# Two interleaved recurrences: the expert layer on blocks of 8 steps, half the lead, and the next stage's first weights spread earlier

## The reference, cut to what matters

```python
def cell(h, x):                                  # layer 1, 256 steps, 8 batches
    gi = x @ W_ih + b_ih; gh = h @ W_hh + b_hh
    r = sigmoid(i_r + h_r); z = sigmoid(i_z + h_z); n = tanh(i_n + r * h_n)
    return (1 - z) * n + z * h
# layer 1's experts, on every h: 8 experts of rank 16, the best one alone
base = h @ W_base.T + b_base;  e = argmax(h @ router_W.T)
x = x + base + 2.0 * B[e] @ (A[e] @ h)
# layer 2, 256 steps: four evaluations a step (Runge-Kutta)
dq = q - q**3/3 - p + x_t + tanh(q) @ coupling.T + bias
dp = EPSILON * (q + ALPHA - BETA * p)
# layer 2's retrieval: 64 of 4096 experts for each row
z = silu((h . down_embed[idx]) * softmax(score));  x = x + sum_k z_k * up_embed[idx_k]
```

## Time and profile before

| | us |
|---|---|
| median of 3 runs | 5199.05 (5195.85 to 5218.25) |
| the profiled execution, its own time | 5227.58 |
| its span, first to last instruction | 5225.8 |
| PE busy | 4851.0 (93%) |
| DVE busy | 2831.0 (54%) |
| ACT busy | 1520.9 (29%) |

### The profile page before, as it was taken

One profiled execution on the slowest core, in us unless ns is written; L12 is line 12 of the kernel. 1 busy time (PEld: TensorE's weight loads), 2 busy tenths in 40 slices (PEclk: granted clock), 3 DMA queues, 4 the chain that ended last, 5 costly groups with the idle time before them and its releaser, 6 DMA issues. The chain is left out here.

```text
span 5225.8 us, 196853 instructions
## 1 busy us (share of the span) xinstructions
PE 4851.0 (93%) x83712; PEld 3836.6 (73%) x83712; DVE 2831.0 (54%) x16413; ACT 1520.9 (29%) x6006; POOL 280.7 (5%) x859
## 2 busy tenths in 40 slices
PE   7899999799999999999996699999989998999978
PEld 3344654589999999999996588799889997344433
DVE  3211011379999999999997635675544341444411
ACT  1100111234444444444443223233322221333310
POOL 0010010001111111111111000000000000000000
PEclk7699999655555555555555599999989999899989
DMA  2201431000000000000001000033400000000000
GB/s 80 101 34 41 165 140 35 14 4 5 5 5 5 5 5 5 5 5 5 5 5 51 13 9 2 34 87 93 128 14 3 3 3 34 11 16 17 12 21 32
DMA packets 54335, 163.72 MB, mean 31 GB/s; under 512 B 13873, under 2 KB 18097, under 8 KB 48192
## 3 DMA queue, kind: packets, MB, share of 16 engines
q1 hardware_dynamic: 47456, 134.89, 7.7%
q0 software_dynamic: 3712, 12.29, 0.7%
q10 hardware_dynamic: 2304, 4.20, 0.2%
HBM read 129.63 MB, written 17.17 MB: 28 GB/s over the span
## 5 line engine op out<-in xcount | busy, mean ns | idle before, releaser
L616 PE MATMUL k_ps<-k_hl,k_wlo 128*128 128x8 f16 x16384 | 606.6, 169 | 141.0 <-ACT k_hl L692 135.9
L616 PEld LDWEIGHTS k_ps<-k_hl,k_wlo 128*128 128x128 f16 x16384 | 532.9, 105 | 178.2 <-ACT k_hl L692 160.6
L620 PE MATMUL k_ps<-k_hl,k_whi 128*128 128x16 f16 x16384 | 588.6, 174 | 0.0
L620 PEld LDWEIGHTS k_ps<-k_hl,k_whi 128*128 128x128 f16 x16384 | 516.1, 104 | 0.6
L616 PE MATMUL g_ps<-g_hl,g_wlo 128*128 128x8 f16 x12288 | 436.7, 168 | 43.2 <-DVE g_hl L770 38.2
L620 PE MATMUL g_ps<-g_hl,g_whi 128*128 128x16 f16 x12288 | 441.5, 174 | 0.0
L616 PEld LDWEIGHTS g_ps<-g_hl,g_wlo 128*128 128x128 f16 x12288 | 387.1, 104 | 49.4 <-DVE g_hl L770 43.6
L692 ACT ACTIVATE k_hl<-k_q 128x32 f16<-128x32 f32 x768 | 176.2, 229 | 742.9 <-DVE k_q L727 742.9
L620 PEld LDWEIGHTS g_ps<-g_hl,g_whi 128*128 128x128 f16 x12288 | 387.1, 104 | 0.0
L1441 DVE TENSOR_REDUCE t_NM<-t_ps 128x1 f32<-128x512 f32 x256 | 165.1, 686 | 218.2 <-PE t_ps L1310 218.2
L1213 DVE TENSOR_TENSOR HQ<-p_ior,p_pm 128x2048 f32<-128x2048 f32 x64 | 146.3, 2290 | 223.7 <-PE p_sim L1037 223.7
(11 more groups left out here) (326 smaller groups left out, 8960.7 us busy)
## 6 DMA issues: line engine op xcount, KB each, us to landing
GRZ<-expert_places SPq DMA_DIRECT2D x64, 512.0 KB, 4.9
wm<-in_w_dram SPq DMA_DIRECT2D x4, 2816.0 KB, 10.4
GRZ<-in_w_dram SPq DMA_DIRECT2D x4, 2816.0 KB, 9.8
m_w<-in_w2a_dram SPq DMA_DIRECT2D x8, 1280.0 KB, 12.7
GRZ<-in_ue_dram SPq DMA_DIRECT2D x8, 1024.0 KB, 8.4
XT<-in_xT_dram SPq DMA_DIRECT2D x1, 4096.0 KB, 12.5
GRZ<-in_x_nat_dram SPq DMA_DIRECT2D x4, 1024.0 KB, 18.8
expert_rows<-wm SPq DMA_DIRECT2D x1, 4096.0 KB, 23.7
```

The source lines that it names most:

```text
L616: T.matmul(P[:,j,1,:],lo[:,kc,(m0+j)*128:(m0+j+1)*128],x[:,kc,0,:],start=(j==0 and kc==0),stop=False,skip_group_check=True)
L620: i=T.matmul(P[:,j,:,:],hi[:,kc,(m0+j)*128:(m0+j+1)*128],x[:,kc,:,:],start=False,stop=kc==KC-1,skip_group_check=True)
```

## The change

The constants become LEAD = 16 and TL = 8. A block of the experts is then 8 steps, 64 rows; there are 32 blocks in place of 16, and each must be through in 8 steps. PE takes four float32 matmuls (eight instructions) a step at i = 0 to 5, where it took two at i = 0 to 11. The matrices in the weights' place stay 128x128 for the base and B matmuls, which now have 64 moving columns; the rank matmuls have 64 weight columns and 136 moving ones. DVE's expert choice moves to i = 1 and 2, its writes of 128x64 to i = 6 and 7, ACT's scaling to i = 3. Step 8(j+1)-16, the first to need block j, comes one step after i = 7; before, it came three steps after i = 13.

In the retrieval tile 0's four is-equal matrices get places of their own (`B0`, in memory that is free by then), so that `weights_hot(0)` is issued on DVE after tile 12's picks, `pairs_hot(0)` after tile 13's, and `pairs_hot(1)` to `(3)` between the last tile's products; PE issues `scatter(0,q)` behind `pick(15,q)`, and ACT `spread(0,q)` there. In the first tile of the second half PE's order becomes `combine(0,q); scatter(1,q)` in place of `scatter(1,q); combine(0,q)`. DVE builds tile 1's matrices in the order 5, 6, 7, 4, then `weights_hot(1)`.

```diff
-LEAD, TL = 32, 16
+LEAD, TL = 16, 8
...
-                if i<2:
-                    if i==0:
-                        e.wait_ge(g_h,TL*(j+1))
...
-                    for d in (2*i,2*i+1):
-                        x=T.matmul(psh[:,0:136],hs[:,d,:],ar[:,d,:],start=d==0,stop=d==3)
-                    if i==1: x.then_inc(l_h,1)
-                if i==2: e.wait_ge(l_x,4*j)
-                if 2<=i<10:
-                    for u in (2*(i-2),2*(i-2)+1):
-                        dc,d=u//4,u%4
-                        T.matmul(pso[:,dc*128:(dc+1)*128],wb[:,d,dc*128:(dc+1)*128],hs[:,d,:],start=u==0,stop=False,skip_group_check=True)
-                if i==4:
+                if i==0:
+                    e.wait_ge(g_h,TL*(j+1))
...
+                    for d in range(4):
+                        x=T.matmul(psh[0:NE,0:136],hs[:,d,:],ar[:,d,:],start=d==0,stop=d==3)
+                    x.then_inc(l_h,1)
+                if i==1: e.wait_ge(l_x,4*j)
+                if 1<=i<5:
+                    dc=i-1
+                    for d in range(4):
+                        T.matmul(pso[:,dc*NE:(dc+1)*NE],wb[:,d,dc*128:(dc+1)*128],hs[:,d,:],start=dc==0 and d==0,stop=False,skip_group_check=True)
+                if i==2:
                     e.wait_ge(l_ht,j+1)
-                    T.transpose(pst[:,0:128],ht[:],K.ident[:]).then_inc(l_tr,1)
-                if i in (10,11):
+                    T.transpose(pst[:,0:NE],ht[0:NE,:],K.ident[0:NE,0:NE]).then_inc(l_tr,1)
+                if i==5:
                     e.wait_ge(l_hm,j+1)
-                    for dc in (2*(i-10),2*(i-10)+1):
-                        x=T.matmul(pso[:,dc*128:(dc+1)*128],bw[:,dc*128:(dc+1)*128],hm[:],start=False,stop=True,skip_group_check=True)
-                    if i==11: x.then_inc(l_o,1)
+                    for dc in range(4):
+                        x=T.matmul(pso[:,dc*NE:(dc+1)*NE],bw[:,dc*128:(dc+1)*128],hm[:,0:NE],start=False,stop=True,skip_group_check=True)
+                    x.then_inc(l_o,1)
...
-                elif i in (12,13):
-                    dc=2*(i-12)+part
+                elif i in (6,7):
+                    dc=2*(i-6)+part
...
+        B0=[x.rearrange('p (j r) -> p j r',r=128) for x in (wm[:,4096:6144],R[:,0:2048],R[:,2048:4096],HF[:,0:2048])]
...
                     pick(i,q)
                     dense(i+1,2*q+1)
+                    if i==NTL-1: scatter(0,q)
...
-            for q in range(4): scatter(0,q)
             for i in range(NTL):
                 for q in range(4):
-                    scatter(i+1,q)
+                    if i>=1: scatter(i+1,q)
                     combine(i,q)
+                    if i==0: scatter(1,q)
...
+                    if i==NTL-1: spread(0,q)
...
                     product(4*i+q)
                     rows_hot(4*i+4+q)
+                    if i==NTL-1 and q<3: pairs_hot(q+1)
...
+                if i==NTL-4: weights_hot(0)
+                if i==NTL-3: pairs_hot(0)
-            for q in range(4): pairs_hot(q)
-            weights_hot(0)
-            for q in range(3): pairs_hot(4+q)
+            for q in range(1,4): pairs_hot(4+q)
+            pairs_hot(4)
             weights_hot(1)
-            pairs_hot(7)
```

More of the change, by code:

```diff
@@ L591, in scan @@
         view=lambda P: P[:,0:64].rearrange('p (m s b) -> p s m b',m=KC,s=2)
-        R_,Z_,N_=range(3)
+        R_,Z_,N_=range(3); NE=TL*NB
         a,h=DT/2,DT
@@ L632, in experts @@
                 hs=HS[:,j%2].rearrange('p d t b -> p d (t b)')
-                if i<2:
-                    if i==0:
-                        e.wait_ge(g_h,TL*(j+1))
-                        if j==0: e.wait_ge(s_lw,64)
-                    for d in (2*i,2*i+1):
-                        x=T.matmul(psh[:,0:136],hs[:,d,:],ar[:,d,:],start=d==0,stop=d==3)
-                    if i==1: x.then_inc(l_h,1)
-                if i==2: e.wait_ge(l_x,4*j)
-                if 2<=i<10:
-                    for u in (2*(i-2),2*(i-2)+1):
-                        dc,d=u//4,u%4
-                        T.matmul(pso[:,dc*128:(dc+1)*128],wb[:,d,dc*128:(dc+1)*128],hs[:,d,:],start=u==0,stop=False,skip_group_check=True)
-                if i==4:
+                if i==0:
+                    e.wait_ge(g_h,TL*(j+1))
+                    if j==0: e.wait_ge(s_lw,64)
+                    for d in range(4):
[7 more added lines that the diff above has]
+                if i==2:
                     e.wait_ge(l_ht,j+1)
-                    T.transpose(pst[:,0:128],ht[:],K.ident[:]).then_inc(l_tr,1)
-                if i in (10,11):
+                    T.transpose(pst[:,0:NE],ht[0:NE,:],K.ident[0:NE,0:NE]).then_inc(l_tr,1)
+                if i==5:
                     e.wait_ge(l_hm,j+1)
-                    for dc in (2*(i-10),2*(i-10)+1):
-                        x=T.matmul(pso[:,dc*128:(dc+1)*128],bw[:,dc*128:(dc+1)*128],hm[:],start=False,stop=True,skip_group_check=True)
-                    if i==11: x.then_inc(l_o,1)
+                    for dc in range(4):
+                        x=T.matmul(pso[:,dc*NE:(dc+1)*NE],bw[:,dc*128:(dc+1)*128],hm[:,0:NE],start=False,stop=True,skip_group_check=True)
+                    x.then_inc(l_o,1)
             for s in range(LEAD):
@@ L680, in masked @@
                 j,i=s//TL-1,s%TL
-                if i!=5 or j<0 or j>=NT//TL: return
-                e.wait_ge(l_tr,j+1); A.activation(hm[:],pst[:,0:128],ACT.Copy,scale=2.0).then_inc(l_hm,1)
+                if i!=3 or j<0 or j>=NT//TL: return
+                e.wait_ge(l_tr,j+1); A.activation(hm[:,0:NE],pst[:,0:NE],ACT.Copy,scale=2.0).then_inc(l_hm,1)
             scaled(0)
@@ L777, in experts @@
                 if j<0 or j>=NT//TL: return
-                if i==2 and part==0:
+                if i==1 and part==0:
                     e.wait_ge(l_h,j+1)
-                    at['mx']=ch.did(V.tensor_reduce(mx[:],psh[:,128:136],AX.X,ALU.max))
-                elif i==2:
[L782 to L787, removed]
+                    at['mx']=ch.did(V.tensor_reduce(mx[0:NE,:],psh[0:NE,128:136],AX.X,ALU.max))
+                elif i==1:
+                    ch.after(at['mx'])
+                    at['mk']=ch.did(V.scalar_tensor_tensor(mk[0:NE,:],psh[0:NE,128:136],mx[0:NE,0:1],io[0:NE,:],ALU.is_ge,ALU.mult))
+                elif i==2 and part==0:
+                    ch.after(at['mk'])
+                    at['ix']=ch.did(V.tensor_reduce(ix[0:NE,:],mk[0:NE,:],AX.X,ALU.min))
+                elif i==2:
                     ch.after(at['ix'])
-                    V.scalar_tensor_tensor(ht[:],io16[:],ix[:,0:1],psh[:,0:128],ALU.is_equal,ALU.mult).then_inc(l_ht,1)
-                elif i in (12,13):
-                    dc=2*(i-12)+part
+                    V.scalar_tensor_tensor(ht[0:NE,:],io16[0:NE,:],ix[0:NE,0:1],psh[0:NE,0:128],ALU.is_equal,ALU.mult).then_inc(l_ht,1)
+                elif i in (6,7):
+                    dc=2*(i-6)+part
                     e.wait_ge(l_o,j+1)
                     x=XT[:,dc,:,j*TL:(j+1)*TL].rearrange('p b t -> p t b')
-                    V.scalar_tensor_tensor(x,pso[:,dc*128:(dc+1)*128].rearrange('p (t b) -> p t b',b=NB),bb[:,dc:dc+1],x,ALU.add,ALU.add).then_inc(l_x,1)
+                    V.scalar_tensor_tensor(x,pso[:,dc*NE:(dc+1)*NE].rearrange('p (t b) -> p t b',b=NB),bb[:,dc:dc+1],x,ALU.add,ALU.add).then_inc(l_x,1)
             e.wait_ge(s_c,32)
@@ L1036, in scatter @@
                         for h in range(2):
-                            x=T.matmul(psw[b][n%2][h*64:(h+1)*64,j*32:(j+1)*32],Bp[b*64:(b+1)*64,q,j,h*64:(h+1)*64],AW[b*64:(b+1)*64,q*16+j,:],start=True,stop=True)
+                            hot=B0[q] if i==0 else Bp[:,q]
+                            x=T.matmul(psw[b][n%2][h*64:(h+1)*64,j*32:(j+1)*32],hot[b*64:(b+1)*64,j,h*64:(h+1)*64],AW[b*64:(b+1)*64,q*16+j,:],start=True,stop=True)
                 x.then_inc(s_W,1)
@@ L1125, in _ @@
             weight(NTL-1)
-            for i in range(NTL):
+            for i in range(1,NTL):
                 for q in range(4): spread(i,q)
@@ L1210, in pairs_hot @@
                 i,q=n//4,n%4
-                if i>=1: e.wait_ge(s_W,n-3)
-                else: e.wait_ge(s_t,4*NTL-3+q)
-                V.tensor_tensor(Bp[:,q],bc(ior[:].unsqueeze(1),[128,16,128]),bc(PM[:,i,1,q*16:(q+1)*16].unsqueeze(2),[128,16,128]),ALU.is_equal).then_inc(s_bp,1)
+                if i==0 and q>=1: e.wait_ge(s_t,4*NTL-3)
+                if i==1: e.wait_ge(s_t,4*NTL)
+                if i==1 and q==0: e.wait_ge(s_W,4)
+                if i>=2: e.wait_ge(s_W,n-3)
+                V.tensor_tensor(B0[q] if i==0 else Bp[:,q],bc(ior[:].unsqueeze(1),[128,16,128]),bc(PM[:,i,1,q*16:(q+1)*16].unsqueeze(2),[128,16,128]),ALU.is_equal).then_inc(s_bp,1)
             def weights_hot(i):
```

## The result

The changed kernel is slower: 5287.59 us median against 5204.41 for the kernel before, measured beside it, ratio 1.016 (95% interval 1.0134 to 1.0186). The forecast was +67 us, to 5266 (5238 to 5302); the medians differ by 83.2.

A forecast was written before the change was run, and what follows sets the result against it. The oscillator's chain was taken to set the scan step, with PE's slot already full. Lead -66.7, new blocks +169, old blocks -18 and retrieval -17 gave +67 us, to 5266 us (5238 to 5302).

The forecast's parts named there:

- The full slot: PE's gap behind the oscillator's fourth evaluation: 0.92 us of room, filled by four instructions (0.99); any more is paid in full.
- The price of an instruction: Expert float32 matmuls in the scan: weight columns set the cost, so it stays 0.213 us at 64 columns and the number doubles.
- the cheap rival: Expert instructions in the scan cost 0.107 us at 64 columns, as moving columns alone would have it; total 5115; chance 0.07.
- The block's excess: Extra time of each new 8-step expert block over steps free of experts: 5.4 us, from 5.0 to 6.1.
- eight narrow instructions: A scan slot holding eight expert instructions lengthens its step by 0.75 to 0.86 us, taken as 0.80.
- The rank portion: Expert instructions at i = 0 of a block, 136 columns at 0.227 us each: 0.88 to 0.98 us extra.
- the transpose: The one PE transpose in each expert block of the scan: 0.21 us extra, as in step 69 before.
- The lead: Sixteen GRU-alone and sixteen oscillator-alone scan steps become sixteen joint ones: 66.7 us gained.
- Waits of POOL: POOL's drive waits for x only one step ahead in the scan; slack covers it, costing nothing, else up to 1 us a block.
- The retrieval: New order in the retrieval brings scatter(2,0) 17 us nearer to the scan's end, from 14 to 20.
- the two later holes: PE gaps of about 5 us in the retrieval that may drop the clock; first combine 8.65 us against some 7.4.
- The sum: Whole kernel: scan +84 and retrieval -17 give +67 us on the median of 5199.05.

The follow-up runs named there:

- half_count: The changed kernel with half of the base matmuls left out, four instructions a slot at i = 1 to 4: scan 2009.7 us against 2106.7.
- half_columns: The changed kernel with base matmuls moving 32 columns in place of 64, half the product left out: scan 2099.1 us against 2106.7.
- wide_transpose: The changed kernel with the transpose of all 128 rows of ht in place of 64: scan 2100.4 us against 2106.7.
- lead32_tl8: The changed kernel with LEAD = 32 and TL = 8, the lead as before: scan 2162.8 us against 2106.7.
- late_ue: The changed kernel with the first four up-embedding pieces issued after two of the last tile's four picks: retrieval 1413.4 us against 1414.0.
- later_ue: The changed kernel with the first four up-embedding pieces issued only after all the last tile's picks: retrieval 1411.6 us against 1414.0.
- lead30_order: The kernel before with LEAD = 30, the changed retrieval, up-embeddings issued behind all picks, and scatter(1,3) ahead of combine(0,3): 5184.97 us, ratio 0.9944.

## Why the prediction was right

The result lies in the range and on the forecast's side, and the mechanism is the one forecast. That the scan's +84 came so near to +84.9 is in part luck: two errors of almost 6 us cancel, as the third step shows. By its steps:

- **The full slot.** Right. half_count takes four instructions out of four slots a block and gets back 97 us.
- **The price of an instruction, 0.213 us at 64 columns.** Right, read from L396 and L117. This was the step on which the sign hung, and the cheap rival fell to half_columns. Its size is twice 128 columns at 1.2 GHz (0.107 us), not once.
- **The block's excess, 5.4 us.** A touch low: steps one to seven of a block stand at 8.34, 8.07, 8.44, 8.03, 8.03, 8.10 and 7.35 in the median (over 7.26), and with the free step the block's excess is 5.6. The 31 new blocks then cost 174.7 us, where I had 167 and 2 for block 0; but the old ones, taken out, had cost 23.6 and not the 18 I took (nor my bound of 23), and -66.2 + 174.7 - 23.6 is 84.9. Of the terms, eight narrow instructions cost 0.75, the bottom of my bounds and not the 0.80 I took. The rank portion cost 1.08 in place of at most 0.98, and the transpose 0.41 in place of 0.21. Both have 64 rows or columns of weights, and I had priced them as if the array size did not matter; wide_transpose shows this for the transpose, and for the rank portion it is argued.
- **The lead, -66.7.** Right: lead32_tl8 forecast 2164 with it, and measured 2162.8. Without the experts' excess the two profiles give -66.2.
- **Waits of POOL.** Right; 0.73 us of slack or more was left.
- **The retrieval, -17.** Mis-sized; it was -6.3. The chain behind it was right (the bare passes over AW cost 4.7 and the clock 2.7), but the step "2 us each" for the scatters between the last picks was wrong. A pick or a scatter takes 2.1 us at the full clock and took 3.6 at the lower one. Up to the last pick that is 7.6 us more, for half a pick, two picks and two scatters, and the hole took 3.2: together 10.8 for the 10.7 by which scatter(1,0) was late. I had allowed for the lower clock in the two later holes alone, and for no hole of PE's own.
- **The sum.** +67 against +83.2 on the medians and +78.6 in the profiles; what is missing in the profiles is the retrieval's 11 us, and the other 4.6 of the medians are no more than executions scatter.

## What to carry to other kernels

Ask of a matmul what it pays for before you cut it up: a float32 instruction with a full set of weights cost 0.213 us at the lower clock with 128, 64 and 32 moving columns alike, so a block of half the rows costs the same and there are twice as many. A shorter lead-in is gained once, while what it takes to allow it is paid in every block: here 56 us once against 141. And where work is packed in the gaps of a full engine, look at the one slot it lands in, not at the busy share.

## What the runs showed of the hardware

- A float32 transpose with 64 rows of weights among full matmuls costs more than a full one: 0.35 + 0.30 us against 0.21 + 0.21 (wide_transpose).
- A row of eight narrow float32 instructions pays for fewer columns once, at its ends, and not eight times: 0.05 us for 32 columns fewer (half_columns).
- PE stopped for 2.8 to 3.2 us with work in hand while the DMA engines were busy with the up-embeddings (the change, late_ue), though for 1.2 us alone in half_columns. With no such transfers under way its holes in the same stage were 0.2 to 1.9 us.
- PE was granted the lower clock while 98% busy with picks and scatters (later_ue, 14.75 of 15 us), and the full one for the same picks and scatters with PE busy for 17.33 of 21.1 us (lead30_order). In the scan it is busy for 1755 of 1800 us and is granted 0.50. Busy time did not tell the clock.
